# Identity products on TensorE at the begin of the first experts and of the second attention

## The chip, the cores and the metric

The program runs on one core of one Trainium2 chip. The metric is the device time of one execution in microseconds (us). A core has TensorE (PE, matmuls; PEld are its weight loads), VectorE (DVE), ScalarE (ACT), GpSimd (POOL) and SyncE (SP), which here only issues DMAs. The engines run their own instruction streams and meet at semaphores.

## The reference

Two layers work on a residual x of 32 batches x 128 tokens x 128 channels, all in float32. Each layer is a cross attention and a mixture of experts:

```
x = x + attention_0(layernorm(x), ctx)      # 16 heads of 8, softmax over 77 keys, masks
x = x + experts_0(layernorm(x))             # 8 experts, 2 of them for each token, silu(x W1) W2, width 512
x = x + attention_1(layernorm(x), ctx)      # rotated q and k, window of 64 keys
x = x + experts_1(layernorm(x))             # 8 experts, 2 of them for each token, width 176, and a shared one
```

## The kernel before

Each engine has one program, written out by hand; nothing is scheduled by a planner. The order on an engine is the order of the calls, and semaphores (`wait_ge`, `then_inc`) tie the engines together. A builder for an attention (`attention`) and one for the experts (`experts`) each give every engine a part; `build` runs them in turn on TensorE: attention 0, experts 0, attention 1 with experts 1 woven into its last steps.

**Attention.** `tensor(pe)` of `attention` runs over steps k. Step k computes the scores of batch k (`scores`, into the four banks of S), turns the softmaxed numbers of batch k-1 (`transpose_group`, ptp), multiplies them with the values (`value_group`, into M0), and turns and projects rows of later batches (`turn_rows` and `products`, in M1). The second attention (`rope` is true) begins at k = -6, but TensorE's first work is `turn_rows(-2)`, which waits for normalised rows: the results of the first experts are loaded by SP, added on GpSimd (lines 463, 465), their statistics taken on VectorE and GpSimd (lines 670, 430 to 433), and normalised on ScalarE (line 542). Then come, on TensorE, `products(-2)`, `turn_rows(-1)`, `products(-1)`, `scores(0)`, `turn_rows(0)`, `products(0)`, `scores(1)`. VectorE takes what `products` gave (lines 768, 769), GpSimd makes the queries of it (line 470), and VectorE runs twice over a batch's scores (lines 790, 791). S is there once, so `scores(n)` waits until both passes over batch n-1 are done.

**Experts 0.** The routed rows of 71 tiles (`SLOTS`) of 128 rows each are read from DRAM into eight buffers (`load`, line 1228). Before the first, SP writes filling rows (line 322) and waits for all scattered rows. On TensorE `take` transposes a tile's rows (line 1384), `widen` multiplies with the first matrix of the tile's expert in four chunks (line 1396), and `narrow` with the second in four (line 1414). ScalarE copies the transposed rows (line 1288) and takes the silu (line 1296); VectorE scales the result (line 1342); GpSimd scatters it (line 1272). The tile's expert is read into a register (`expert`), after `take(0)` and `take(1)` for the first two.

TensorE's last work ahead of these are keys and values of the second attention, projected early (lines 931, 933, 943); ScalarE copies them out (lines 516, 517, 522). `keys_copied` waits for the copies of the keys.

Places touched: in `experts` the line before `take(0)`, in bank 2 of S, whose first 128 columns are the transposed rows of `take` and whose last 128 nobody uses there; in `attention` the line before the wait for `masks_set`, in the same columns, and behind `products(k)`, in the last 128 columns of M0, which hold nothing before `turn_output(0)`.

Of the kernel before, what the change touches and what calls it, by code (L numbers as in the profile page):

```python
# [43 lines left out]
C_ID, C_HM, C_BAND, C_COS, C_SIN = 0, 128, 136, 216, 344  # L44
# [54 lines left out]
def live(n):  # L99

    return 0 <= n < B
# [37 lines left out]
def turned_rows(layer, k):  # L139

    if k > B:
        return {B + 1: [B - 4, B - 3], LAST_TURN[layer]: [B - 2, B - 1]}.get(k, [])
    return [k - 5] if live(k - 5) else []
# [9 lines left out]
def sent_in(layer):  # L153

    plan, queue = {}, []
    for k in range(B + 6):
        for g, (b0, size, _, _) in enumerate(GROUPS_AT[layer]):
            if RANK_AT[layer][g] == k - 1:
                queue += range(b0, b0 + size)
        if k < B - 8 or layer and k < B - 3:  # L160
            take = 1
        else:
            take = len(queue) if k > B + 1 else 1 if k == B + 1 else 2 if layer or k % 2 == 0 else 1
        plan[k], queue = queue[:take], queue[take:]
    return plan


class Steps:
# [18 lines left out]
def attention(nc, st, layer, w):  # L187
# [7 lines left out]
    rope = layer == 1  # L195
# [10 lines left out]
    x, cst, identb = st["x"], st["cst"], st["identb"]  # L206
    ident = cst[:, C_ID:C_ID + 128]
# [42 lines left out]
    S, ptp, M0, M1 = sh["S"], sh["ptp"], sh["M0"], sh["M1"]  # L250
# [55 lines left out]
    def wait(eng, s, value):  # L306

        if value > 0:
            eng.wait_ge(s, value)
# [626 lines left out]
    def project_values(pe, c):  # L936

        if not rope and c < 2:
            pe.wait_ge(k_copied, KCH)
        wait(pe, v_copied, c - 1)  # L940
        for t in range(VB):
            n = c * VB + t
            last = nc.tensor.matmul(ptp[c % 2][0:TK, t, :], ctxT[:, n * TK:(n + 1) * TK], wt["v"], start=True, stop=True)
        last.then_inc(v_ready, 1)
# [15 lines left out]
    def tensor(pe):  # L960
# [40 lines left out]
        def turn_output(n):  # L1001
            pe.wait_ge(ot_copied, n + 1)
            for s in range(2):
                last = nc.tensor.transpose(O[:, s * T:(s + 1) * T], OTs[:, s, :], ident)  # L1004
            last.then_inc(o_ready, 1)
# [16 lines left out]
        def ranks(g):  # L1022

            size = groups[g][1]
            pe.wait_ge(both_ready, g + 1)
            nc.tensor.matmul(rankp[:, 0:size * E], beforeb[:, :], both[:, 0:size, :], start=True, stop=False, skip_group_check=True)
            for b in range(size):
                after = size - b
                last = nc.tensor.matmul(rankp[:, (b + 1) * E:(size + 1) * E], onesb[:, :],
                                        both[:, b:b + 1, :].broadcast_to([128, after, E]), start=False,  # L1030
                                        stop=(b == size - 1), skip_group_check=True)
            return last

        def products(k):


            if k < B + 2 or k == LT:
                wait(pe, turned_copied, min(k, B + 2) + 3)
            else:
                pe.wait_ge(products_taken, k + 2)  # L1040
            if live(k - 2):
                nc.tensor.matmul(Y, aT, wt["o"], start=True, stop=False)  # L1042
                last = nc.tensor.matmul(Y, st["three"][:, :], bo, start=False, stop=True)
            if live(k + 2):
                last = nc.tensor.matmul(Qp, wt["q"], xT, start=True, stop=True)  # L1045
                if rope:
                    last = nc.tensor.matmul(Qrp, wt["qr"], xT, start=True, stop=True)
            for at, _ in enumerate(turned_rows(layer, k)):
                last = nc.tensor.matmul(lgp[:, at * E:(at + 1) * E], xrT[at], st["Wg"][layer][:, :], start=True, stop=True)
            if k in RANK:  # L1050
                last = ranks(RANK.index(k))
            last.then_inc(products_ready, 1)
# [8 lines left out]
        pe.wait_ge(st["consts_in"], st["n_consts"])  # L1061
        pe.wait_ge(st["ident_ready"], 1)
        if rope:
            pe.wait_ge(masks_set, 1)
        for k in range(START, B + 1):
            a = k - 1
            if not rope and -4 <= k < 0:
                if k == -1:
                    pe.wait_ge(mv_set, 3)
                    pe.wait_ge(masks_set, 2)  # L1070
                    nc.tensor.matmul(M0[:, 0:B], keepA[:, :], keepP[:, :], start=True, stop=True).then_inc(counts_ready, 1)
                project_values(pe, 2 * k + 8)
                project_values(pe, 2 * k + 9)
            if live(k - 2):
                turn_output(k - 2)
                if not rope and k == 2:
                    pe.wait_ge(st["bias_in"], 16)
            if live(k):
                scores(k)
            if live(a):  # L1080
                transpose_group(a, 0)
                transpose_group(a, 1)
            if -2 <= k:
                turn_rows(k)
            if live(a):
                transpose_group(a, 2)
                transpose_group(a, 3)
                value_group(a, 0)
                value_group(a, 1)
                value_group(a, 2)  # L1090
                value_group(a, 3)
            if -2 <= k:
                products(k)
            yield k
        for step in TAIL:
            if step == "divide":
# [28 lines left out]
def experts(nc, st, layer, w, maps_set, x_updated):  # L1125

    two = layer == 1
# [14 lines left out]
    three, x, cst, emap, rowmap = st["three"], st["x"], st["cst"], st["emap"], st["rowmap"]  # L1142
    ident = cst[:, C_ID:C_ID + 128]
# [8 lines left out]
    S = sh["S"]  # L1152
# [22 lines left out]
    def wait(eng, s, value):  # L1175

        if value > 0:
            eng.wait_ge(s, value)
# [33 lines left out]
    def of_expert(t, e):  # L1212

        if isinstance(e, int):
            return t[:, e, :]
        return t[:, bass.ds(e, 1), :].rearrange("p a f -> p (a f)")
# [159 lines left out]
    def tensor(pe):  # L1376
        pe.wait_ge(st["weights_in"], st["n_weights"])
        pe.wait_ge(st["bias_in"], 16)

        def take(n):  # L1380

            pe.wait_ge(xs_in[n % U], 16 * (n // U) + 16)
            wait(pe, xsT_copied, n)
            nc.tensor.transpose(xTp, xs[:, n % U, 0:D], ident).then_inc(xsT_ready, 1)  # L1384

        def widen(n, e):

            pe.wait_ge(xsT_copied, n + 1)
            if two:
                wait(pe, hb_ready, n - 1)  # L1390
                nc.tensor.matmul(up[n % 2][:, 0:UW], xsT[:, n % 3, :], of_expert(W1, e), start=True, stop=False)  # L1391
                nc.tensor.matmul(up[n % 2][:, 0:UW], three[:, :], of_expert(w["B1"], e), start=False, stop=True).then_inc(up_ready, 1)  # L1392
                return
            pe.wait_ge(w1_copied, n + 1)
            for c in range(FC):
                last = nc.tensor.matmul(hTp[n % 2][:, c, :], w1s[:, n % 2, c * 128:(c + 1) * 128], xsT[:, n % 3, :],  # L1396
                                        start=True, stop=True)
            last.then_inc(hT_ready, 1)

        def turn_hidden(n):  # L1400

            pe.wait_ge(h_ready, n + 1)
            wait(pe, hT_copied, n)
            for c in range(FC):
                last = nc.tensor.transpose(hTp[0][:, c, :], h[:, n % 2, c * 128:(c + 1) * 128], ident)  # L1405
            last.then_inc(hT_ready, 1)

        def narrow(n, e):

            pe.wait_ge(hT_copied, n + 1)  # L1410
            wait(pe, ys_ready, n)
            w2 = W2[:, e, :, :] if isinstance(e, int) else W2[:, bass.ds(e, 1), :, :].rearrange("p a c d -> p (a c) d")
            for c in range(FC):
                last = nc.tensor.matmul(yp, hT[:, n % 2, c, :], w2[:, c, :], start=(c == 0), stop=(c == FC - 1))  # L1414
            last.then_inc(yp_ready, 1)

        take(0)
        take(1)
        if not two:
            maps_set(pe)  # L1420
        of = {0: expert(pe, 0), 1: expert(pe, 1)}
        late = 3 if two else 1
        for n in range(NS + late):
            if live(n):
                widen(n, of[n])
            if live(n + 2):
                take(n + 2)
                if two and n + 2 == FIRST:
                    maps_set(pe)
                of[n + 2] = expert(pe, n + 2)  # L1430
            if two and live(n - 2):
                turn_hidden(n - 2)
            if live(n - late):
                narrow(n - late, of.pop(n - late))
            yield n
# [225 lines left out]
```

## Time and profile before

| | us |
|---|---|
| median of 3 executions | 861.1 |
| lowest and highest | 859.41, 865.08 |
| the profiled execution | 855.94 |
| its span, first to last instruction | 854.1 |

The profiled execution was timed apart from the three. The span leaves out 1.8 us around the instructions. A transpose is a matmul instruction with the transposed matrix as weights. "PEclk" and the clock in windows are the granted TensorE clock as a share of 2.4 GHz: 1.00 is 2.4 GHz, 0.50 is 1.2 GHz. A matmul record is an instruction that the profiler saw, each with its own weight load (LDWEIGHTS, on PEld). A row of the timeline merges neighbours of one line: its duration runs from the first one's start to the last one's end, and since the records overlap, their pace is read from start to start.

### The profile page before, as it was taken

How to read it: one execution, taken by the hardware profiler on the slowest of the kernel's cores; microseconds unless marked ns; L12 is line 12 of the kernel's file. 1: busy time of each engine (PE TensorE's matmuls, PEld its weight loads, DVE VectorE, ACT ScalarE, POOL GpSimd, SP SyncE). 2: the span in 40 equal slices, each digit the busy share in tenths (PEclk: the TensorE clock that was granted, in tenths of full speed). 3: DMA queues.
4: the chain of work that ended last, by engine and by line, in shares of the span. 5: the costliest groups of instructions: out<-in, count | busy, mean ns of one | idle time of the engine just before them, and what ended most of it. 6: DMA issues, size and time to landing. Idle time of an engine off the chain costs nothing.

```text
span 854.1 us, 21614 instructions
## 1 busy us (share of the span) xinstructions
PE 760.0 (89%) x7159; PEld 594.2 (70%) x7159; DVE 509.9 (60%) x1598; ACT 440.1 (52%) x1136; POOL 505.9 (59%) x897
## 2 busy tenths in 40 slices
PE   5899998899993999999399999999877599999994
PEld 3677676666663999999267777777655377776773
DVE  2678886886751654444167798999764433333336
ACT  4466564554662333344146566565537256665662
POOL 6433665767563666666664457788565517666630
PEclk9999999998996999999679999999979889999998
DMA  7800000000012222221210111212012312222258
GB/s 223 338 2 2 21 21 18 23 27 28 26 55 71 73 74 70 71 70 58 63 32 26 39 35 46 61 43 58 27 42 68 88 39 83 78 81 76 76 145 220
DMA packets 65408, 57.62 MB, mean 67 GB/s; under 512 B 10547, under 2 KB 58675, under 8 KB 64758
## 3 DMA queue, kind: packets, MB, share of 16 engines
q1 hardware_dynamic: 56662, 38.27, 16.2%
q0 software_dynamic: 8640, 17.97, 6.2%
q8 instruction: 62, 1.02, 0.5%
q14 instruction: 44, 0.36, 0.2%
HBM read 34.03 MB, written 24.20 MB: 68 GB/s over the span
## 4 chain that ended last, share of the span: by engine, by line
PE 58%; POOL 12%; issue 9%; DVE 6%; ACT 4%; another core or an unknown queue 3%; DMA 2%; SPq 1%; POOLq 0%; DVEq 0%
PE ptp L985 13%; POOL results L1272 9%; PE M L996 7%; PE S L1391 6%; PE ptp L1414 6%; PE S L971 5%; PE S L973 5%; PE M L1042 2%; PE S L1405 2%; ACT pT L568 2%; PE M L1004 2%; POOL xi L1265 2%; PE M L1045 2%; PE S L1392 2%
## 5 line engine op out<-in xcount | busy, mean ns | idle before, releaser
L568 ACT ACTIVATE pT<-ptp 77x512 f32<-77x512 f32 x256 | 140.2, 589 | 151.0 <-PE ptp L985 132.9
L1272 POOL DMA_INDIRECT results<-early,xi x142 | 149.4, 1052 | 96.2 <-DVE early L1342 92.6
L491 POOL DMA_INDIRECT rows<-out_rows,posi x128 | 127.6, 997 | 63.0 <-issue 32.0
L985 PE MATMUL ptp<-cst,pr 128*77 128x128 f32 x1024 | 145.0, 285 | 5.5 <-ACT pT L568 2.8
L985 PEld LDWEIGHTS ptp<-cst,pr 128*77 128x77 f32 x1024 | 120.2, 152 | 22.7 <-ACT pT L568 12.7
L1288 ACT ACTIVATE early<-S 128x128 f32<-128x128 f32 x174 | 48.3, 277 | 163.4 <-PE S L1384 81.5
L1334 DVE TENSOR_TENSOR hw<-hw,S 128x176 f32<-128x176 f32 x103 | 34.7, 337 | 110.1 <-issue 59.7
L790 DVE TENSOR_REDUCE mx<-S 128x16 f32<-128x1232 f32 x64 | 91.3, 1427 | 13.2 <-PE S L973 12.2
L791 DVE TENSOR_TENSOR pr<-S,mx 128x1232 f32<-128x1232 f32 x64 | 92.2, 1441 | 2.2
L1391 PE MATMUL S<-W,early 128*128 (+1 forms) x206 | 80.8, 475 | 0.0
L1414 PE MATMUL ptp<-W,early 128*128 (+1 forms) x412 | 72.0, 299 | 8.9 <-DVE x_res L1347 5.1
L996 PE MATMUL M<-pT,vm 77*32 77x128 f32 x2048 | 77.5, 281 | 1.4 <-ACT pT L568 1.1
L1414 PE MATMUL S<-first_w,early 128*128 x568 | 76.6, 278 | 1.8 <-ACT early L1296 0.9
L1396 PE MATMUL S<-early,w1s 128*128 128x128 f32 x568 | 76.5, 279 | 0.6 <-ACT early L1288 0.6
L430 POOL TENSOR_TENSOR negm<-zero,mv 128x4 f32<-128x4 f32 x40 | 8.0, 200 | 110.1 <-DVE mv L673 105.2
L1414 PEld LDWEIGHTS S<-first_w,early 128*128 128x128 f32 x568 | 68.9, 191 | 3.4 <-issue 2.9
L1396 PEld LDWEIGHTS S<-early,w1s 128*128 128x128 f32 x568 | 70.6, 195 | 0.9 <-ACT early L1288 0.9
L1414 PEld LDWEIGHTS ptp<-W,early 128*128 128x128 f32 x412 | 55.3, 195 | 17.5 <-issue 9.0
L1342 DVE TENSOR_SCALAR early<-S,xs 128x128 f32<-128x128 f32 x71 | 24.9, 351 | 69.5 <-PE S L1414 55.5
L996 PEld LDWEIGHTS M<-pT,vm 77*32 77x32 f32 x2048 | 48.5, 110 | 23.4 <-ACT pT L568 12.5
L1384 PE MATMUL S<-cst,xs 128*128 128x128 f32 x174 | 48.5, 279 | 16.6 <-DMA xs<-rows 11.6
L971 PE MATMUL S<-kexp,qT 32*128 32x308 f32 x512 | 54.6, 497 | 4.1 <-POOL kexp L443 2.1
(162 smaller groups left out, 1488.9 us busy)
## 6 DMA issues: line engine op xcount, KB each, us to landing
xs<-rows SPq DMA_DIRECT2D x142, 66.0 KB
first_w<-in_e_W SPq DMA_DIRECT2D x2, 2048.0 KB, 10.3
swap<-results SPq DMA_DIRECT2D x32, 128.0 KB
first_w<-results SPq DMA_DIRECT2D x8, 512.0 KB, 7.4
results<-early,xi POOLq DMA_INDIRECT x142
rows<-out_rows,posi POOLq DMA_INDIRECT x128
rows<-out_rows SPq DMA_DIRECT2D x32, 64.0 KB
xs<-rows SPq DMA_DIRECT2D x32, 64.0 KB
```

Source lines behind the costliest of these rows:

```text
L491: nc.gpsimd.indirect_dma_start(rows[:, :], bass.IndirectOffsetOnAxis(posi[:, k, n:n + 1], 0), out_rows[:, ring_slot(groups, n), k, :], Non ...
L568: nc.scalar.activation(pT[:, r, :, :], ptp[r % 2][0:TK, :, :], ACT.Exp, scale=SCALE).then_inc(exp_done, 1)
L790: do(V.tensor_reduce(mx[:, :].rearrange("p (g j) -> p g j", g=G), sc, AX.X, ALU.max))
L791: V.tensor_tensor(pr[:, n % 2, :, :].rearrange("p (g j) k -> p g j k", g=G), sc, mx[:, :].rearrange("p (g j) -> p g j", g=G).unsqueeze(3). ...
L971: nc.tensor.matmul(S[:, g, 0:GK], qT[heads, n % 2, :], kexp[heads, n % 2, :, :], start=True, stop=False)
L985: last = nc.tensor.transpose(ptp[r % 2][0:TK, j, :], pr[:, n % 2, r * J + j, :], ident)
L996: last = nc.tensor.matmul(OT[32 * j:32 * j + 32, s * T:(s + 1) * T], vm[:, n % 2, at:at + 32], pT[:, r, j, :], start=(r == 0), stop=(i == ...
L1272: nc.gpsimd.indirect_dma_start(results[:, :], bass.IndirectOffsetOnAxis(xi[:, s:s + 1], 0), ys[:, s, :], None)\
L1384: nc.tensor.transpose(xTp, xs[:, n % U, 0:D], ident).then_inc(xsT_ready, 1)
L1391: nc.tensor.matmul(up[n % 2][:, 0:UW], xsT[:, n % 3, :], of_expert(W1, e), start=True, stop=False)
L1396: last = nc.tensor.matmul(hTp[n % 2][:, c, :], w1s[:, n % 2, c * 128:(c + 1) * 128], xsT[:, n % 3, :], start=True, stop=True)
L1414: last = nc.tensor.matmul(yp, hT[:, n % 2, c, :], w2[:, c, :], start=(c == 0), stop=(c == FC - 1))
```

## The change

A function `keep_warm` multiplies the 128x128 float32 identity by itself a given number of times, into the last 128 columns of a PSUM bank. Nothing reads them. It is called with 84 ahead of the first transposes of experts 0, with 84 at the begin of the second attention, and with 5, 4 and 16 behind `products(-2)`, `products(-1)` and `products(0)` there: 193 products. It adds no wait of its own; nothing else is added, removed or moved, and the other engines' programs are the same.

```
+SPARE = slice(384, 512)
+WARM_AT = {-2: 5, -1: 4, 0: 16}
+
+
+def keep_warm(nc, st, bank, count):
+    ident = st["cst"][:, C_ID:C_ID + 128]
+    for _ in range(count):
+        nc.tensor.matmul(bank[:, SPARE], ident, ident, start=True, stop=True, skip_group_check=True)
@@ attention, tensor(pe)
         pe.wait_ge(st["ident_ready"], 1)
         if rope:
+            keep_warm(nc, st, st["shared"]["S"][:, 2, :], 84)
             pe.wait_ge(masks_set, 1)
@@
             if -2 <= k:
                 products(k)
+            if rope and k in WARM_AT:
+                keep_warm(nc, st, M0, WARM_AT[k])
             yield k
@@ experts, tensor(pe)
             last.then_inc(yp_ready, 1)
 
+        if not two:
+            keep_warm(nc, st, st["shared"]["S"][:, 2, :], 84)
         take(0)
         take(1)
```

Below is the order of TensorE's program as written, where a float32 product counts once (line numbers of the second kernel are 10 or 13 higher). At the begin of the first experts, before; ptp takes the last value projections, `S<-cst,xs` are the transposes of `take`:

```order
L931 MATMUL S<-early,W 128x154
L933 MATMUL S<-early,W 128x154
L943 MATMUL ptp<-W,early 77x128 x12
L1384 MATMUL S<-cst,xs 128x128 x2
L1209 TENSOR_LOAD emap x2
L1396 MATMUL S<-early,w1s 128x128 x4
```

The same place now; `S<-cst` are identity products:

```order
L941 MATMUL S<-early,W 128x154
L943 MATMUL S<-early,W 128x154
L953 MATMUL ptp<-W,early 77x128 x12
L175 MATMUL S<-cst 128x128 x84
L1397 MATMUL S<-cst,xs 128x128 x2
L1222 TENSOR_LOAD emap x2
L1409 MATMUL S<-early,w1s 128x128 x4
```

Between the value projections and the first transposes there are now 84 products.

At the begin of the second attention on TensorE, before; `M<-cst,xn` are the transposes of `turn_rows`, `M<-turned,W` the products of `products`, and the lines onto S the scores:

```order
L1414 MATMUL S<-first_w,early 128x128
L1016 MATMUL M<-cst,xn 128x128
L1045 MATMUL M<-turned,W 128x128
L1047 MATMUL M<-turned,W 128x128
L1016 MATMUL M<-cst,xn 128x128
L1045 MATMUL M<-turned,W 128x128
L1047 MATMUL M<-turned,W 128x128
L971 MATMUL S<-kexp,qT 128x308 x4
L973 MATMUL S<-bandb,identb 128x308 x4
L1016 MATMUL M<-cst,xn 128x128
L1045 MATMUL M<-turned,W 128x128
```

The same place now:

```order
L1427 MATMUL S<-first_w,early 128x128
L175 MATMUL S<-cst 128x128 x84
L1026 MATMUL M<-cst,xn 128x128
L1055 MATMUL M<-turned,W 128x128
L1057 MATMUL M<-turned,W 128x128
L175 MATMUL M<-cst 128x128 x5
L1026 MATMUL M<-cst,xn 128x128
L1055 MATMUL M<-turned,W 128x128
L1057 MATMUL M<-turned,W 128x128
L175 MATMUL M<-cst 128x128 x4
L981 MATMUL S<-kexp,qT 128x308 x4
L983 MATMUL S<-bandb,identb 128x308 x4
```

There are 84 products ahead of the first transpose, 5 and 4 behind the first two projections, and 16 more behind the third, ahead of the scores of batch 1.

## Rows read from the trace of the kernel before

**Rows 1.** The page: busy time of TensorE, and the clock in 40 slices.
```profile
PE 760.0 (89%) x7159; PEld 594.2 (70%) x7159; DVE 509.9 (60%) x1598; ACT 440.1 (52%) x1136; POOL 505.9 (59%) x897
...
PEclk9999999998996999999679999999979889999998
```

**Rows 2.** Windows: stretch, its length, TensorE's busy time and records, clock, DMA.
```profile
256.00:260.00 4.00, 0.84 (x8) 0.91 0.52 143
...
412.00:414.00 2.00, 0.00 (x0) 0.73 0.10 33
414.00:416.00 2.00, 0.00 (x0) 0.50 0.65 193
...
436.00:438.00 2.00, 1.92 (x13) 0.80 0.00 0
```

**Rows 3.** Timeline, begin of the first experts: start, duration, operation, count [idle before].
```profile
253.80 3.04 PE L943 MATMUL ptp<-W,early 128*77 128x128 f32 x24
...
267.81 0.45 PE L1384 MATMUL S<-cst,xs 128*128 128x128 f32 x1 [10.97 <-DMA xs<-rows]
...
268.78 0.45 PE L1384 MATMUL S<-cst,xs 128*128 128x128 f32 x1 [0.52 <-ACT early L1288]
...
269.82 2.05 PE L1396 MATMUL S<-early,w1s 128*128 128x128 f32 x8 [0.59 <-ACT early L1288]
...
271.66 0.42 PE L1384 MATMUL S<-cst,xs 128*128 128x128 f32 x1
...
272.41 1.28 ACT L1296 ACT_TABLE_LOAD   x1
...
273.71 0.60 ACT L1296 ACTIVATE early<-S 128x512 f32<-128x512 f32 x1
...
274.46 1.15 PE L1414 MATMUL S<-first_w,early 128*128 x8 [0.90 <-ACT early L1296]
```

**Rows 4.** Timeline, end of the first experts and begin of the second attention.
```profile
409.01 1.15 PE L1414 MATMUL S<-first_w,early 128*128 x8 [0.71 <-DVE early L1342]
...
420.95 0.45 PE L1016 MATMUL M<-cst,xn 128*128 128x128 f32 x1 [10.78 <-ACT xn L542]
```

**Rows 5.** Timeline, the first two batches of the second attention.
```profile
423.68 0.48 PE L1016 MATMUL M<-cst,xn 128*128 128x128 f32 x1 [0.70 <-DVE swap L769]
...
426.39 0.46 POOL L470 TENSOR_TENSOR qT<-swap 128x128 f32<-128x128 f32 x1
...
426.90 1.41 PE L971 MATMUL S<-kexp,qT 32*128 32x308 f32 x8 [0.64 <-POOL qT L470]
...
428.24 0.64 PEld L973 LDWEIGHTS S<-bandb,identb 128*128 128x128 bf16 x4 [0.82 <-issue]
428.25 1.21 PE L973 MATMUL S<-bandb,identb 128*128 128x308 bf16 x4
...
430.97 1.44 DVE L791 TENSOR_TENSOR pr<-S,mx 128x1232 f32<-128x1232 f32 x1
...
432.55 1.41 PE L971 MATMUL S<-kexp,qT 32*128 32x308 f32 x8 [1.30 <-DVE pr L791]
```

**Rows 6.** Timeline of TensorE, scores of batches 2 and 3.
```profile
440.13 0.80 PE L971 MATMUL S<-kexp,qT 32*128 32x308 f32 x8
...
446.07 0.80 PE L971 MATMUL S<-kexp,qT 32*128 32x308 f32 x8
```

**Rows 7.** Timeline of an expert tile, and all records of lines 1396 and 985 (durations ns).
```profile
283.03 1.06 PE L1396 MATMUL S<-early,w1s 128*128 128x128 f32 x8
...
284.93 1.06 PE L1396 MATMUL S<-early,w1s 128*128 128x128 f32 x8
...
L1396 PE MATMUL S<-early,w1s x568: 275/275/553, 269.8 to 407.1; 128*128 128x128 f32 x190
...
L985 PE MATMUL ptp<-cst,pr x1024: 270/273/494, 30.0 to 643.3; 128*77 128x128 f32 x171
```

**Rows 8.** Windows: busy time and records of PE, PEld, DVE, ACT, POOL; clock, DMA.
```profile
450.00:600.00 150.00, 148.20 (x1790) 111.99 (x1779) 133.61 (x405) 91.26 (x196) 102.17 (x198) 1.00 0.15 44
```

## The prediction

> **What bounds the kernel now.** I read the page's busy times and its clock line first [rows 1], then the two stretches where TensorE stands still, by windows [rows 2], then the timeline through both [rows 3 to 6]. TensorE is busy for 760.0 of 854.1 us. The clock line is 9 nearly throughout, and its dips are few: the change addresses two of them. In windows the reader sees the same course twice. The last matmul ends at 256.84 and 410.16 us; no matmul follows for 11 us; in between the granted clock falls from 1.00 (2.4 GHz) to 0.50 (1.2 GHz), a mean of 0.91 at 256 to 260 and of 0.73 at 412 to 414, some 2.4 and 2.8 us after the last matmul [rows 2]. So the waits leave TensorE at 1.2 GHz when its next work comes.
>
> Outside them TensorE sets the pace. In the first experts one tile (17 matmul records) follows the next every 1.90 us without a gap [rows 7]; in the second attention TensorE is busy for 148.2 of 150 us, VectorE for 133.6 [rows 8]. What is added to TensorE there in excess of a wait is therefore paid in full, and so is what a faster TensorE gives back.
>
> **What one filler product costs.** This decides the case. The filler is float32, 128x128 by 128x128, start and stop set, and not a transpose. The nearest rows have exactly this shape: the first product of an expert, line 1396, four of them a tile for 71 tiles, is 284 products, and the trace counts 568 records [rows 7]: each float32 product runs as two, each with a weight load of its own. Transposes (line 985: 16 a batch, 64 batches, x1024 in the trace) are one record each [rows 7]. The pace of such records at 2.4 GHz is that of the expert tile: from 283.03 to 284.93 us lie 17 of them, 0.112 us each; at 1.2 GHz the eight at 269.82 take until 271.66 with one transpose behind them, 0.21 to 0.23 each [rows 3, 7]. So a filler product costs 2 x 0.112 = 0.223 us at the full clock, and 84 of them 18.8 us. At both places the wait has room for about 11.
>
> That the stationary operand is the identity again and again saves nothing that a row shows: the mask products (line 973) are four in a row with the same identity, and each has its own load [rows 5].
>
> The Trainium skill, page "TensorE: Matmul & The Clock Gate", section "Back-to-back issue gap", gives about 81 ns for one LDWEIGHTS and MATMUL pair of 128 columns. By that figure 84 fillers would be an estimated 6.8 us and fit the wait. The rows of this kernel disagree by their number: two pairs a product, 112 ns a pair. The sum goes by the rows.
>
> **Place 1, begin of the first experts.** The last value projection ends at 256.84 us, and a record lasts 0.27 and lets the next begin after 0.11, so the filler starts near 256.7: what it waits for besides is done (the copies of the keys stand ahead of those of the values on ScalarE; weights and bias are loaded in the first attention) [rows 3]. It ends issuing at 256.7 + 18.8 = 275.5. The first transpose of an expert's rows started at 267.81, when its DMA had come [rows 3]. It is queued behind the filler: +7.7 us.
>
> Given back: from this transpose to the first second product (line 1414) it was 274.46 - 267.81 = 6.65 us, partly at 1.2 GHz [rows 3]. At 2.4 GHz: transpose 0.27 for 0.45, copy, second transpose at 0.8, the gap of 1.04 us to the first weight load of line 1396 that I leave (two table values are read into registers there), eight records 0.89 for 1.84, third transpose 0.27, copy 0.28, ScalarE's table load 1.28 (which hides under nothing), its activation 0.60. That puts line 1414 at 5.45 us: -1.2 us. What follows already ran at 2.4 GHz and bound by TensorE. Place 1: +6.5. That the eight row loads, the indices and the weights' copies are now all ready earlier helps nothing, since none was waited for after 269.82.
>
> **Place 2, begin of the second attention.** The last product of the experts starts at 409.01, eight records, so the filler starts at 409.9 and ends issuing at 428.7. The first transpose (line 1016) started at 420.95 [rows 4]: +7.7 us. The other engines use the delay to prepare two batches' rows, no more, as their buffers are double.
>
> Given back, counted from that transpose: before, scores of batch 0 at +5.95, of batch 1 at +11.60, of batch 2 at +19.18 us (440.13), from which the clock is full and the rhythm is 5.94 us a batch [rows 5, 6]. After: the step k=-2 takes transpose 0.27, copy 0.28, four records 0.60, and VectorE's two operations 0.6, so its result is there at +1.9; the five fillers (ten records, 1.1 us) hold TensorE until +2.2, 0.3 beyond it. k=-1 then ends at +3.3 for TensorE, four fillers bring +4.2; the scores of batch 0 stand there instead of at +5.95, since GpSimd's work before them (line 470) was done during the delay. They take 1.44 us for 2.56. VectorE's passes over them end 2.95 us after the scores (429.46 to 432.41, line 791 the second [rows 5]), at +8.6. TensorE has its transpose and four records until +6.6, and then sixteen fillers, 32 records, 3.6 us, until +10.2: here too the filler is longer than the wait, by 1.6. Scores of batch 1 at +10.2 (11.6 before), of batch 2 one iteration at full clock later, 5.6: +15.8 instead of +19.2. Given back: 3.4. Place 2: +4.3.
>
> **The sum.** 7.7 - 1.2 + 7.7 - 3.4 = +10.8 us. The profiled execution took 855.94 us (854.1 span and 1.8 around it), so its like is 866.7. That execution is 5.2 us below the median of the three timed; on that median it is 861.1 + 10.8 = 872. Bounds of what is returned: nothing, or half of all that lies before the clock is back, 3.3 of the 6.65 us of place 1 and 7.9 of the 15.8 us from 420.95 to 436.8 (the window of 436 to 438 has a mean of 0.80 [rows 2]). That puts the sum between +4.2 and +15.4.
>
> **Rivals.**
> *The filler is half as long* (it comes out on the other side). If TensorE ran an identity product as one record, as it does a transpose, 84 took 9.4 us and ended at 266.1 and 419.3, both inside the wait; 5, 4 and 16 would fill 0.56, 0.45 and 1.8 us. The wait decides at 11.1 us / 84 = 0.132 us a product. Then only the returns are left: 1.2 at place 1, and at place 2, where GpSimd again sets the scores of batch 0 to 426.90, 1.3 us on each of the scores of batches 0 and 1 that hide under nothing, less an overlap, 2.9 together: 857. For it: the counts fit the waits of 0.70, 0.64 and 1.30 us [rows 5]. Against it: every float32 product that isn't a transpose has two records here [rows 7]. 5%. The Trainium skill's 81 ns a pair would lie on this rival's side of the 0.132 us, if a product were one pair.
>
> *The delay is absorbed.* While TensorE runs filler, GpSimd, VectorE, ScalarE and the row loads get ahead by up to 7.7 us; if the batches or tiles that follow were bound by one of them, the excess would come back. That asks for slack on TensorE, and there is 1.8 us of it in 150 [rows 8]; later dips of the clock line (from 600 us on [rows 1]) may fall otherwise, either way. It would give 862 to 868. 13%.
>
> *The clock falls all the same,* within the filler or after it. At 1.2 GHz 168 records of 0.21 to 0.23 us are 36 to 38 us, so both places would cost some 17 us more each: above 900. The filler starts 0.1 us after real work at a granted clock of 1.00, and real records at the same pace held it at 1.00 for over 100 us. 2%.
>
> **How the numbers follow.** The forecast has 80%: 872, by itself 867 to 878. No change that a measurement can tell is within 1%, 8.6 us: the forecast's lower part (its bounds, and medians that moved between 859.4 and 865.1), most of the second rival and half of the first lie there, 27%. Faster by more than 1% needs the first rival and luck, 4%; slower 69%. The range, 862 to 879, leaves out the first and the last rival and the forecast's edges.
>
> **What the profile would show.** Line 175 with x386 records (2 x 193) and pairs 0.22 us apart; a right count of x193 would make the first rival right. The filler from 256.7 to 275.5 and from about 416 to 435 on the shifted clock axis; the transpose of line 1397 directly behind, with no idle time before it, and the wait put down to nothing. PEclk at 1.00 through both, where windows showed 0.50. Line 1414's successor (1427) 5.4 us behind the first transpose, scores of batch 2 15.8 us behind the first transpose of the attention, and before batch 1's scores sixteen fillers that end after VectorE's subtraction. If the wait before the first real transpose is still there, the prediction is wrong by its first step; if later batches come faster than 5.94 us or tiles faster than 1.90, by its second.

## The result, and the profile after

The changed kernel took 876.7 us (median of 6, 874.31 to 878.38), the kernel before 860.0 beside it (857.12 to 865.08): ratio 1.0214, 95% interval 1.0173 to 1.0254. The forecast was 872 in a range of 862 to 879, ratio 1.013: the side and the range held, and the change was +16.7 us where +10.8 was forecast, some 6 more. The profiled executions are 873.8 and 854.1 us of span, 19.7 apart. All medians here and below are of all executions; the ratios with their intervals leave out those that were over 1.5% slower than the fastest of the same kernel. From the page of the changed kernel, the lines that answer to [rows 1]:

```profile
span 873.8 us, 22385 instructions
...
PE 798.8 (91%) x7545; PEld 634.4 (73%) x7545; DVE 511.2 (58%) x1598; ACT 440.1 (50%) x1136; POOL 506.2 (58%) x897
...
PEclk9999899999999999999999999999989889999997
```

TensorE has 386 records more, 38.8 us more busy time, and the two dips of the clock line in the middle are gone. What was aimed at was reached, and the kernel is slower. All records of the new line, with the shortest, median and longest duration in ns:

```profile
L175 PE MATMUL S<-cst x336: 269/275/423, 256.6 to 440.5; 128*128 128x128 f32 x168
...
L175 PE MATMUL M<-cst x50: 275/275/275, 441.8 to 451.0; 128*128 128x128 f32 x50
```

84 + 84 products are 336 records, 25 are 50: two a product, as the expert rows said [rows 7]. The timeline of TensorE at the first experts, to be read against [rows 3]:

```profile
253.68 3.04 PE L953 MATMUL ptp<-W,early 128*77 128x128 f32 x24
256.56 4.28 PE L175 MATMUL S<-cst 128*128 128x128 f32 x36
261.33 0.36 PE L175 MATMUL S<-cst 128*128 128x128 f32 x1 [0.49 <-issue]
263.52 0.38 PE L175 MATMUL S<-cst 128*128 128x128 f32 x2 [1.83 <-issue]
264.27 16.29 PE L175 MATMUL S<-cst 128*128 128x128 f32 x129 [0.36 <-issue]
280.39 0.27 PE L1397 MATMUL S<-cst,xs 128*128 128x128 f32 x1
...
285.84 1.15 PE L1427 MATMUL S<-first_w,early 128*128 x8 [1.37 <-ACT early L1309]
```

GpSimd, which reads the same buffer of rows and has no filler ahead of it, shows in its own timeline when they came:

```profile
268.89 0.19 POOL L1278 TENSOR_TENSOR xi<-xs,zero 128x1 uint32<-128x1 uint32 x1 [6.53 <-DMA xs<-rows]
```

The reader is to see three things. The first real transpose stands directly behind the filler, with no wait, 11.5 us after GpSimd read its rows. Line 1427 follows it after 5.45 us (6.65 before). And the filler is interrupted: after 36 records TensorE stands still, waiting for nothing but "issue", runs one record at 261.33 and two from 263.52, and goes on at 264.27. It took 23.8 us, not 18.8. The windows (columns as in [rows 2]) show that the clock fell behind the pause, to 0.50 from 265.2 to 268.6, in the middle of the filler:

```profile
260.00:264.00 4.00, 1.59 (x10) 1.00 0.37 85
264.00:268.00 4.00, 3.73 (x21) 0.65 0.16 38
268.00:272.00 4.00, 4.00 (x35) 0.93 0.30 70
```

The second attention, against [rows 4 to 6]:

```profile
420.82 1.15 PE L1427 MATMUL S<-first_w,early 128*128 x8 [0.71 <-DVE early L1355]
421.81 18.92 PE L175 MATMUL S<-cst 128*128 128x128 f32 x168
440.57 0.27 PE L1026 MATMUL M<-cst,xn 128*128 128x128 f32 x1
...
445.05 0.80 PE L981 MATMUL S<-kexp,qT 32*128 32x308 f32 x8
...
447.51 3.74 PE L175 MATMUL M<-cst 128*128 128x128 f32 x32
451.18 0.80 PE L981 MATMUL S<-kexp,qT 32*128 32x308 f32 x8
...
456.86 0.80 PE L981 MATMUL S<-kexp,qT 32*128 32x308 f32 x8
```

Here the filler runs without a break and the transpose again stands behind it without a wait. The sixteen end at 451.2, and the scores of batch 1 follow at once, without a wait. VectorE's passes, which ended the wait in the kernel before [rows 5], were over at 449.44, 1.7 us earlier, by VectorE's timeline:

```profile
448.00 1.44 DVE L801 TENSOR_TENSOR pr<-S,mx 128x1232 f32<-128x1232 f32 x1
```

The same marks, read from the timelines of all traces, give the stages (us). "Wait 1" is from the last record of the value projections to the first transpose of the experts, "back 1" from there to the first second product, "tiles" on to the last tile's (0.1 us behind the start of its eight records), "wait 2" on to the attention's first transpose, "b2" from there to the scores of batch 2, "rest" on to the end of the span. The last column groups the traces by the chip on which they ran (empty where it was not noted).

| kernel | start | wait 1 | back 1 | tiles | wait 2 | b2 | rest | span | chip |
|---|---|---|---|---|---|---|---|---|---|
| before | 256.6 | 11.24 | 6.65 | 134.7 | 11.84 | 19.18 | 414.0 | 854.1 | |
| before_again | 260.3 | 9.25 | 6.66 | 134.8 | 11.90 | 19.63 | 408.6 | 851.1 | 8 |
| changed | 256.5 | 23.94 | 5.45 | 135.1 | 19.66 | 16.29 | 416.9 | 873.8 | |
| half | 254.0 | 11.91 | 5.46 | 134.7 | 13.14 | 19.51 | 417.5 | 856.3 | 6 |
| transposes | 256.7 | 12.62 | 5.46 | 134.6 | 12.75 | 17.12 | 417.8 | 857.1 | 6 |
| first_only | 260.3 | 21.68 | 5.49 | 134.5 | 12.00 | 18.88 | 409.0 | 861.8 | 6 |
| second_only | 255.9 | 7.55 | 6.68 | 134.3 | 19.65 | 16.30 | 415.4 | 855.8 | 6 |
| fitted | 255.8 | 9.75 | 5.50 | 135.1 | 12.96 | 17.25 | 411.4 | 847.7 | 10 |
| late_filling | 255.6 | 19.68 | 5.58 | 134.8 | 19.66 | 16.28 | 414.3 | 865.9 | 10 |
| bf16 | 259.3 | 12.03 | 5.51 | 135.1 | 12.49 | 18.24 | 418.1 | 860.7 | 10 |
| second_bare | 256.7 | 11.68 | 6.65 | 134.9 | 19.66 | 14.91 | 423.9 | 868.5 | 10 |
| fitted_steps | 240.7 | 8.12 | 5.51 | 135.5 | 13.72 | 16.18 | 398.4 | 818.1 | 2 |
| after_again | 240.9 | 18.86 | 5.49 | 133.3 | 19.66 | 16.28 | 395.0 | 829.5 | 2 |
| double | 240.7 | 37.62 | 5.46 | 133.3 | 38.42 | 16.29 | 397.4 | 869.2 | 2 |

The 19.7 us between the first and the third row are +12.7 at wait 1, -1.2 at back 1, +0.4 in the tiles, +7.8 at wait 2, -2.9 at b2, and +3.0 in the rest, less 0.1 at the start. The spans of different rows also differ by what is ahead of the change (start: 240.7 to 260.3) and by the rest; so a theory about a place is judged by its stage, and a whole kernel by the timed ratio to the kernel before on the same chip.

### The profile page after: what moved, and what is told of

Its sections match the earlier page's. It is cut to its first block, busy times and chain, and to the rows that moved or that the text cites. A ratio compares the mean times of both kernels' runs of the same rounds, so it can differ in the third digit from the quotient of the medians.

```text
span 873.8 us, 22385 instructions
## 1 busy us (share of the span) xinstructions
PE 798.8 (91%) x7545; PEld 634.4 (73%) x7545; DVE 511.2 (58%) x1598; ACT 440.1 (50%) x1136; POOL 506.2 (58%) x897
## 4 chain that ended last, share of the span: by engine, by line
PE 78%; ACT 4%; DVE 4%; issue 3%; another core or an unknown queue 3%; DMA 2%; POOL 1%; SPq 0%; DVEq 0%; ACTq 0%; POOLq 0%
PE ptp L995 14%; PE S L1427 8%; PE M L1006 7%; PE S L1409 7%; PE ptp L1427 5%; PE S L1404 5%; PE S L981 5%; PE S L175 5%; PE S L983 4%; PE M L1052 2%; PE S L1418 2%; PE S L1397 2%; PE M L1014 2%; PE M L1055 2%
## 5 line engine op out<-in xcount | busy, mean ns | idle before, releaser
L995 PEld LDWEIGHTS ptp<-cst,pr 128*77 128x77 f32 x1024 | 119.9, 151 | 23.9 <-ACT pT L578 11.7
L800 DVE TENSOR_REDUCE mx<-S 128x16 f32<-128x1232 f32 x64 | 91.3, 1427 | 14.1 <-PE S L983 13.6
L1427 PE MATMUL ptp<-W,early 128*128 (+1 forms) x412 | 73.4, 303 | 10.8 <-DVE x_res L1360 6.8
L1006 PEld LDWEIGHTS M<-pT,vm 77*32 77x32 f32 x2048 | 47.9, 109 | 22.8 <-ACT pT L578 11.7
L786 DVE TENSOR_TENSOR x_res<-x_res,M 128x128 f32<-128x128 f32 x64 | 18.5, 289 | 60.7 <-PE M L1059 25.1
```

The costliest lines, as they stand in the source:

```text
L800: do(V.tensor_reduce(mx[:, :].rearrange("p (g j) -> p g j", g=G), sc, AX.X, ALU.max))
L995: last = nc.tensor.transpose(ptp[r % 2][0:TK, j, :], pr[:, n % 2, r * J + j, :], ident)
L1006: last = nc.tensor.matmul(OT[32 * j:32 * j + 32, s * T:(s + 1) * T], vm[:, n % 2, at:at + 32], pT[:, r, j, :], start=(r == 0), stop=(i == ...
```

## The experiments

**Half the counts, and transposes for products.** `half` has 42 and 42, and 2, 2, 8; `transposes` keeps the counts and multiplies as a transpose:

```
-            keep_warm(nc, st, st["shared"]["S"][:, 2, :], 84)      # both places
+            keep_warm(nc, st, st["shared"]["S"][:, 2, :], 42)
-WARM_AT = {-2: 5, -1: 4, 0: 16}
+WARM_AT = {-2: 2, -1: 2, 0: 8}
```
```
-        nc.tensor.matmul(bank[:, SPARE], ident, ident, start=True, stop=True, skip_group_check=True)
+        nc.tensor.transpose(bank[:, SPARE], ident, ident)
```

> Half of every count: 42 and 42 products, and 2, 2, 8 behind the steps (96 products, 192 records). Theory 1, a product is two records of 0.112 us and what exceeds a wait is paid in full: each 42 take 9.4 us and end inside the waits of 11 us, the first real transpose of each place starts where it did in the kernel before (about +11.1 us after the last real matmul), and only the returns are left, 1.2 us at the first experts and 2.9 to 3.4 at the attention: 4 us below the kernel before, ratio 0.995. Rival: the pause of 3.4 us inside the first filler (260.84 to 264.27 in the changed kernel) belongs to the program position of the 37th record; then it comes again, the filler ends near 271 and place 1 loses 3 us more than it did before: ratio 1.00. Rival 2: the filler disturbs the other engines or DMAs by itself; then the first transposes start later than in the kernel before although the filler has ended.

> The same counts (84, 84, 5, 4, 16), but each is a transpose of the identity, one record in place of two. In time it is the half filler: 9.4 us a place, ended inside the waits. Theory 1 (a transpose keeps the clock as a product does): as the half filler, 4 us below the kernel before, clock 1.00 through both places. Rival (the clock does not count transposes as activity): the clock falls to 0.50 during the filler, the transposes then take 0.21 us each, 84 of them up to 15 us, so each place is entered at 0.50 and 2 to 4 us late: 3 to 8 us above the kernel before.

Measured: half 855.3 against 855.6, ratio 0.998 (0.994 to 1.002); transposes 858.9, ratio 1.002 (0.997 to 1.006). Both are within noise of the kernel before: with the filler about as long as the waits, or shorter, the loss of 2% is gone, which is the first theory's main claim. Its 4 us of gain did not come. Half, timeline of TensorE at both places:

```profile
254.14 3.62 PE L175 MATMUL S<-cst 128*128 128x128 f32 x31
258.07 0.27 PE L175 MATMUL S<-cst 128*128 128x128 f32 x1 [0.31 <-issue]
259.48 0.36 PE L175 MATMUL S<-cst 128*128 128x128 f32 x1 [1.15 <-issue]
260.25 5.86 PE L175 MATMUL S<-cst 128*128 128x128 f32 x51 [0.41 <-issue]
265.94 0.27 PE L1397 MATMUL S<-cst,xs 128*128 128x128 f32 x1
...
407.03 9.54 PE L175 MATMUL S<-cst 128*128 128x128 f32 x84
419.28 0.30 PE L1026 MATMUL M<-cst,xn 128*128 128x128 f32 x1 [2.71 <-ACT xn L552]
```

Half, windows at and behind the end of the second filler (columns as in [rows 2]):

```profile
416.00:420.00 4.00, 0.92 (x8) 0.94 0.22 66
420.00:424.00 4.00, 2.97 (x12) 0.50 0.22 66
```

The pause came again, behind 31 records and for 2.4 us, and made the half filler 11.8 us, so that even it ended behind the rows' arrival (GpSimd read them at 263.38). At place 2 the filler ended 2.7 us before the transpose, and the clock fell at 419.5, with the first real work: nothing was gained there (b2 19.5). The second rival's sign came too: that transpose was 13.1 us behind the last product, and 11.8 to 12.0 without a filler there (before, before_again, first_only). The delay lies between GpSimd's last scatter and its first addition, while the scatter lands and SP's loads run. But it isn't a filler's rule: the normalised rows (ScalarE's first xn) were ready 11.2 to 11.5 us behind the start of the last eight product records with no filler at place 2 and in all five traces with 84 float32 products there, and at 12.0 to 13.2 in half, transposes, fitted, bf16, fitted_steps and double. Its cause is open. The transposes, one record each, show the rival about them wrong: a filler of nothing but transposes held the clock at 1.00. Its timeline of TensorE, and then its windows over the same stretch:

```profile
410.30 9.33 PE L175 MATMUL S<-cst 128*128 128x128 f32 x84
422.16 0.30 PE L1026 MATMUL M<-cst,xn 128*128 128x128 f32 x1 [2.52 <-ACT xn L552]
```
```profile
414.00:418.00 4.00, 4.00 (x39) 1.00 0.45 131
418.00:422.00 4.00, 1.63 (x15) 1.00 0.23 66
```

In the kernel before, the clock had fallen 2.8 us after the last matmul [rows 2]; here it stayed up for the 9.2 us of the filler and fell only at 423.2, one us after the real work had begun, with 2.5 us of idleness ahead of that. The Trainium skill, page "TensorE: Matmul & The Clock Gate", section "Part 4: PE-mode transpose", says that transposes do not count as activity as matmuls do; the granted clock of this run, 1.00 over all 9.2 us of them, does not agree.

**One place alone.** `first_only` takes out the calls in the attention, `second_only` the one in the experts.

> 84 products ahead of the first experts alone, nothing at the attention. Theory 1: place 1 costs by itself 7.7 us of excess and gives back 1.2; with the pause inside the filler and the clock that falls behind it 5.1 us more, so the step from the last value projection to the first experts' second product is +11.5 us; the attention then has its old wait of 11.9 us from the last product to the first transpose. About 11 us above the kernel before. If the pause does not come again, about 6.5. Rival: the places are not independent, and the old attention wait is shorter than before because other engines are ahead.

> No filler at the first experts, 84 and 5, 4, 16 at the attention. Theory 1: place 1 as in the kernel before (first transpose of the experts 11 us after the last projection), place 2 +7.8 us of excess up to its first transpose and 2.9 given back until the scores of batch 2: about 5 us above the kernel before at that point. Rival: the pause inside a filler comes at any place; then place 2's filler takes 22 us or more here as well.

The places are independent: wait 1, back 1 of first_only are 21.7 and 5.5 with wait 2 at its old 12.0, and wait 2, b2 of second_only are 19.65 and 16.30 with back 1 at its old 6.7. First_only took 863.6 us in its one execution, 8.0 above the kernel before on the same chip, where about 11 was expected: wait 1 and back 1 together are 9.3 us longer than in the first trace of the kernel before, not 11.5, mostly since the clock stayed at 1.00 behind the pause. Second_only took 857.7, 2.1 above, with +7.8 and -2.9 at its stages as expected. The pause came at place 1 (2.8 us, behind 31 records), never at place 2. Something not foreseen: without a filler, wait 1 was 7.55 us here, 11.24, 11.68 and 9.25 in three other traces. The excess at place 1 has no fixed size; what went with it is shown under the next run.

**The pause.** `late_filling` moves SP's writes of filling rows (`fill_up`) behind the wait for all scattered rows, in both expert layers.

> The changed kernel with one thing moved: SP writes the filling rows only after all rows have been scattered (it wrote them at the same time). The pause in the first filler began 31 to 36 records after its begin in four traces, and SP stood still in the same stretch, with steps at the same moments. Theory A (the pause is the filling rows' and the scatters' writes at the same time holding back both engines' instruction flow): the pause moves from 260.6 to 264.3 to behind the last scatter or vanishes. Theory B (it belongs to the 32nd record or to the place in the program): it stays 31 to 36 records behind the filler's begin and is as long. In both the excess stays, about 17 us above the kernel before, since TensorE is the last at place 1 unless the filling rows now end after it.

Timeline of TensorE in late_filling, and then that of SP's queue:

```profile
255.74 19.20 PE L175 MATMUL S<-cst 128*128 128x128 f32 x168
275.31 0.33 PE L1397 MATMUL S<-cst,xs 128*128 128x128 f32 x1 [0.37 <-DMA xs<-rows]
```
```profile
263.66 7.63 SPq L332 DMA_DIRECT2D rows<-in_filling  x8
```

No pause (the widest step is 0.3 us), the filler is 19.0 us long, and SP issues its eight writes in 7.6 us. The rows came only at 275.3, so here TensorE even waited for them a little. The one execution took 867.8 us, 7.0 above the kernel before on the same chip, and not about 17 as expected. Its stages up to b2 are 12.4 us longer than in the first trace of the kernel before, and the filler of 19.0 us in place of 23.8, which the expectation did not reckon with, is about half of what was missed. SP's queue in the changed kernel, and then in `after_again`, where the same eight took 10.8 and 7.7 us:

```profile
253.41 10.80 SPq L332 DMA_DIRECT2D rows<-in_filling  x8
```
```profile
236.28 7.71 SPq L332 DMA_DIRECT2D rows<-in_filling  x8
```

And SP's queue without any filler at place 1, in the kernel before and then in second_only:

```profile
253.41 11.15 SPq L322 DMA_DIRECT2D rows<-in_filling  x8
```
```profile
250.38 8.03 SPq L332 DMA_DIRECT2D rows<-in_filling  x8
```

So SP is held up with or without a filler, and where it wasn't, in second_only, the wait was the shortest, 7.55 us. From the first of the eight writes to the last it took 9.2 to 11.6 us in 19 of the 20 stretches (two layers, ten traces) outside chip 2 in which scatters were issued beside them. The exception is the first layer of second_only, 7.6. In late_filling and on chip 2 all eight stretches took 7.1 to 7.4.

That speaks for theory A: with the filling rows and GpSimd's scatters in flight together, SP and TensorE both stand still for a few us, in the changed kernel with steps at the same moments (SP's next instructions at 261.29, 262.00, 263.51 and 264.23, TensorE's weight loads at 261.32, 262.04, 263.53 and 264.25). Neither does it alone: in late_filling the filler ran beside the scatters until 261.5 and beside the filling rows after 263.7. Theory B is out by the same run, and by chip 2, where the order of the changed kernel ran without the pause. The records in front of it number 27 to 36 in six traces, also with bfloat16 records at half the spacing. That would fit a queue in front of TensorE that holds about so many when its supply stops, which no run here shows. For TensorE's pause theory A rests on one execution with the streams apart; what exactly holds the engines back, and why not on chip 2 and not in second_only, stays open.

**The type of the product.** `bf16` multiplies `identb`, the bfloat16 identity.

> The same counts of products, but of the bfloat16 identity. Theory: a bfloat16 product is one record, so the 84 are 84 records; by the one bfloat16 row with this operand (four of 308 columns in 0.70 us, 0.13 to 0.17 us each) and fewer columns they come every 0.06 to 0.11 us and take 5 to 9.4 us, so they end 2.5 to 7 us before the first real transpose, and the clock falls before the real work: place 2 is entered at 0.50 or falls at its first steps, and the time is that of the kernel before within 3 us. Rival: the pace is bound by the weight load at 0.11 us whatever the type, 9.4 us, and it behaves as the transposes did.

Timeline of TensorE at the second place, and then a window of the same kernel there:

```profile
412.76 4.85 PE L175 MATMUL S<-identb 128*128 128x128 bf16 x84
424.36 0.45 PE L1026 MATMUL M<-cst,xn 128*128 128x128 f32 x1 [6.75 <-ACT xn L552]
```
```profile
420.00:424.00 4.00, 0.00 (x0) 0.58 0.23 69
```

84 records for 84 products, 0.056 us apart, a quarter of the float32 product's cost. The filler ended 6.8 us early and the attention began at 0.50, and the one execution took 862.5 us, 1.7 above the kernel before, all as expected. At place 1 wait 1 was 12.0, with a longer pause (5.7 us).

**The small fillers.** `second_bare` has 84 at the attention alone and `WARM_AT = {}`.

> 84 products at the begin of the attention alone, without the 5, 4 and 16 behind its first steps. Theory: the scores of batch 0 stand 4.2 us behind the first transpose (4.5 with the small fillers) and, above all, those of batch 1 wait for VectorE's passes alone, 8.7 to 9.0 us behind it, instead of 10.6 with the sixteen; batch 2 follows 5.7 us later, 14.5 instead of 16.3. The clock stays at 1.00. So the small fillers cost 1.6 to 2 us. Rival: without them the clock falls within the first two batches, and the scores of batch 2 come 17 us or more behind the first transpose.

Timeline of TensorE, the scores of batches 1 and 2:

```profile
433.04 0.80 PE L981 MATMUL S<-kexp,qT 32*128 32x308 f32 x8
...
437.57 0.80 PE L981 MATMUL S<-kexp,qT 32*128 32x308 f32 x8 [1.91 <-DVE pr L801]
```

Batches 0, 1, 2 stand at 3.4, 7.9 and 14.9 us, against 4.5, 10.6 and 16.3 with the small fillers: 1.1 us for the five and four, 1.6 for the sixteen. Without them the clock did fall, at 438.4 for 3.4 us, and batch 2 came 7.0 us behind batch 1, not 5.7; it was still 1.4 us earlier. So the small fillers do cost time, 1.4 us at batch 2 where 1.6 to 2 was expected, and batches 0 and 1 came 0.8 us or more sooner than worked out, batch 2 0.4 later; that the clock stays up without them is wrong, but its fall did not cost what the rival said.

**The price of a product, and the changed kernel again.** `double` has 168 and 168; `after_again` is the changed kernel.

> 168 and 168 products in place of 84 and 84, 5, 4, 16 as they were. Theory (the excess is paid in full, 0.223 us a product, and other engines' lead brings nothing back): each place is 18.8 us longer than in the changed kernel, 37.5 us in all, about 911 to 915. The stages behind each place are as long as before. Rival (the delay is in part absorbed by what others prepare meanwhile): less than 35 us more, with shorter tiles or batches behind.

> The changed kernel once more, beside the others. Theory: the same stages as in its first trace: the first filler interrupted after 31 to 36 records for about 3 us, 23 to 24 us in all, and the second uninterrupted, 18.8 us; ratio to the kernel before 1.017 to 1.025. Rival: the pause in the first filler was of that one execution; then the ratio is about 1.013.

Timelines of TensorE, double and then after_again:

```profile
240.81 37.68 PE L175 MATMUL S<-cst 128*128 128x128 f32 x336
278.32 0.27 PE L1397 MATMUL S<-cst,xs 128*128 128x128 f32 x1
```
```profile
241.04 18.92 PE L175 MATMUL S<-cst 128*128 128x128 f32 x168
259.80 0.27 PE L1397 MATMUL S<-cst,xs 128*128 128x128 f32 x1
```

On this chip the kernel before took 816.9 us, and the ratio of after_again is 1.019 (1.015 to 1.022), 14.4 us. Wait 1 and wait 2 of double are each 18.76 us longer than in after_again, 0.2233 us a product, and every stage behind is as long (133.3, 5.5, 16.3, and the rest 2.4 longer): paid in full, nothing absorbed. Double took 871.0 us in its one execution, 39.6 above the changed kernel where 37.5 was expected. The absolute 911 to 915 was missed, since the kernel before is 5% faster on this chip. That isn't spread evenly: of the 44 us between the two traces of the changed kernel 16 lie before the change is reached, 5 in wait 1 and 22 in the rest, while the tiles are only 1% shorter and wait 2 and b2 are the same. The expectation of after_again was wrong in an instructive way: the pause did not come, and the ratio is nearly the same. fitted_steps on the same chip had its rows 8.1 us after the projections. By that wait the excess at place 1 is 18.9 - 8.1 = 10.8 us, without a pause, and 23.9 - 11.2 = 12.7 with one. By GpSimd's reading of the rows in the traces themselves, 9.1 and 12.4 us after the projections, it is 9.7 and 11.5. With the pause both are longer, the filler and the wait for the rows, since SP, which has to issue the loads of the rows, is held up as well.

**Counts fitted to the waits.** `fitted` has 30, 52 and {3, 3, 8}; `fitted_steps` 30, 52 and {9, 4, 7}.

> Counts cut to the waits that the traces show: 30 products at the first experts (6.7 us and the pause of 2.5 to 3 us inside), 52 at the attention (11.6 us; the wait from the last product to the first transpose was 11.8 to 13.1 us in five traces), 3, 3 and 8 behind the steps. Theory (the excess was the whole loss, and a filler that ends 2.9 us too early lets the clock fall just as the work begins, as half the counts did at the attention): no excess at either place, clock at 1.00 through both, 1.2 us given back at the experts and about 3 at the attention: ratio 0.995, 4 us. Rival: what is given back there is lost again in the last batches and the second experts, where the clock's dips fall differently from run to run: ratio 0.998 to 1.002.

> As the fitted counts (30 and 52), but 9, 4 and 7 behind the steps instead of 3, 3 and 8. In the fitted run the clock fell 5.5 us behind the filler's end, at 424.0, in the middle of the attention's first steps, since ScalarE's copy of the second step waits for GpSimd and TensorE has little to do there. Theory: six more products behind the first step lie in that wait and keep the clock at 1.00 until the scores of batch 2, which then stand 16 to 16.5 us behind the first transpose (17.3 with 3, 3, 8 and 19.2 in the kernel before). Whole kernel 0 to 5 us below the kernel before, which the spread of the executions, some 8 us, lets show only in part. Rival: the nine hold up the second step, and its scores come later than 5.95 us behind the first transpose.

Fitted 860.9 against 860.9, ratio 1.002 (0.997 to 1.007); fitted_steps 816.9 against 816.9, ratio 1.000 (0.998 to 1.003). The stages are near what was wanted: back 1 at 5.5, b2 at 17.3 and 16.2. In fitted the clock fell for 3.4 us at 424.0, in the attention's first steps, which was not expected. The nine products in fitted_steps ended that, and its scores of batch 0 were not later than before (5.96 us). From the projections to the scores of batch 2 fitted took 180.5 us, the kernel before 183.6 and 182.2. That is 2 to 3 us, of it up to 1.5 by the wait at place 1 that differs anyway, and the whole kernel does not show it. Three reasons can be seen. Wait 2 was 1.1 us longer in fitted, and 13.7 in fitted_steps, as described for half above. In fitted_steps the clock fell at 251.9, 3.1 us behind the first real transpose, although the filler had ended only 1.2 us before that one, and the first tiles ran at 1.2 GHz (tiles 135.5, against 133.3 in the two others of this chip, 2.2 us). Windows of fitted_steps:

```profile
248.00:252.00 4.00, 1.98 (x13) 0.99 0.34 81
252.00:256.00 4.00, 3.45 (x17) 0.50 0.23 59
```

And the rest varies more than the gain: 408.6 and 414.0 us in the two traces of the kernel before, 409.0 without a filler at place 2, 411.4 to 423.9 in the eight traces with one outside chip 2. The dips of the clock in the last batches and at the begin of the second experts differ in number and place from trace to trace. Whether the filler at place 2 makes them worse, or the traces only look like it, is open. No version was measurably faster than the kernel before.

**The kernel before once more**, for the size of what no edit explains.

> The kernel before once more, for the spread of its own stages. Theory: the last product of the experts' tiles to the scores of batch 2 of the attention is 31 us and the tiles 133 to 135 us, as in its first trace; the wait at the first experts differs (7.5 to 11.7 us in traces without a filler there), and the end, from the scores of the last batch on, differs by several us with nothing changed (224 us in its first trace, 225 to 234 in those of the variants). Rival: the end is 224 again, and what the changed kernel lost there, 3.8 us, is its own.

It took 852.9 us, and a further execution on the same chip 859.7. The stages of its trace are in the table: wait 1 is 9.25 us where it was 11.24, and the rest 408.6 where it was 414.0, with nothing changed. Cut at the scores of the last batch, the stretch ahead of them (from those of batch 2) is 184.4 us where it was 189.7, and the one behind is 224.2 us where it was 224.3. So in these two traces the kernel's own variation lies in the middle batches, and the end is as long, as the rival said. In the changed kernel the two are 188.9 and 228.1, in fitted 185.4 and 226.0, in second_bare 189.8 and 234.1, in first_only 184.0 and 225.0: outside chip 2 the end is 1.7 to 10 us longer with a filler at place 2 (eight traces), and 0.7 without one (first_only). That speaks for a cost far behind the filler, but doesn't show it: only three traces are without a filler there, and on chip 2 the end was 218.2, 214.7 and 217.2 us in three kernels that all have one. No mechanism was found.

## Why the prediction was right, and where its size was off

- *A product costs two records, 0.223 us.* Right: 386 records, and 18.76 us for 84 by double. The first rival is out by the same count. The Trainium skill, page "TensorE: Matmul & The Clock Gate", section "Back-to-back issue gap", gives 81 ns a pair, and that is not this kernel's: a float32 pair takes 112 ns, a bfloat16 pair 56.
- *Place 1, +7.7 of excess.* This is the term that was mis-sized: it was +12.7 in the profiled execution. The filler was taken at 18.8 us and took 23.8 (3.3 us of standing still and 1.8 lost at 1.2 GHz behind it; by late_filling the two DMA streams together go with it). The forecast said of this place that the filler starts after real work at full clock and so keeps it; it was not asked whether TensorE's instructions keep coming. Where there is no pause, the wait itself was shorter and the excess 9.7 to 10.8. The wait was taken from one execution, and without a filler it varies from 7.5 to 11.7 us.
- *Given back 1.2 at place 1.* Right, 1.20 (6.65 to 5.45).
- *Place 2, +7.7, and 3.4 given back.* +7.8 and 2.9. The scores stood at 4.5, 10.6 and 16.3 us where 4.2, 10.2 and 15.8 were worked out. The fillers' part in it, that the sixteen outlast VectorE's passes by 1.6 us, is read from VectorE's timeline and shown by second_bare.
- *The rest unchanged.* It was 3.0 us longer; the kernel before differs from itself by 5.4 there, so this term is not explained.
- *The second rival, absorption.* Out by double. *The third, that the clock falls all the same:* it did, for 3.4 us behind the pause, at a cost of 1.8 us and not of 17, so the sign "PEclk at 1.00 through both" failed at place 1. A pause need not bring it: the clock stayed at 1.00 behind pauses of 2.8 us (first_only) and 3.3 us (transposes).

The sum by the terms as measured is 12.7 - 1.2 + 7.8 - 2.9 = 16.4 us without tiles and rest, beside 16.7 between the medians. That they agree so closely is in part luck, as wait 1 alone differs by 4 us between traces without a filler. The side was no luck: both fillers outlast their waits for the reason forecast, two records a product, and double shows the price.

## What to carry to other kernels

Price a filler by records of its own type and shape, and count the records a product makes: float32 makes two here, and 84 for a wait with room for 50 or 36 turned an expected gain of 4 us at most, which no version showed, into a loss of 17. A filler of fixed length stands in the program of the engine that everybody waits for, so it must be shorter than the shortest wait seen in several executions; where it ends too early the clock may fall all the same (half, bf16), and what it has beyond the wait is paid in full (double). Ask first what the clock gives back: here 1.2 and 3 us, less than the kernel differs from itself.

## What the runs showed of the hardware

- With two DMA streams in flight together (SP's eight writes of filling rows, DRAM to DRAM, and GpSimd's scatters) SP took 9.2 to 11.6 us for its writes in place of 7.1 to 7.6, and TensorE stood still for 2.4 to 5.7 us, behind 27 to 36 records of the filler. It came in all six traces with a filler beside both streams on the other chips, in none of three on chip 2, and not when the streams were one after the other (late_filling, one execution).
- Transposes alone held the granted clock at 1.00 for 9 us.
- The clock also fell with TensorE at work in small pieces: at 424.0 in fitted and 251.9 in fitted_steps, with waits of under 2 us between real records, and at 438.4 in second_bare.
- One chip ran the same kernel before in 816.9 us, where the medians on the others were 855.6 to 861.
